# A graph kernel's first gathers, moved from the start of message passing into the attention answers

## The chip, the cores and the metric

The kernel runs on 1 core of one Trainium2 chip. The metric is the device time of the core in microseconds; lower is better. TensorE is called PE in the profile (its weight loads PEld), VectorE is DVE, ScalarE is ACT, GpSimd is POOL, and SP is the engine that issues the plain transfers.

## The reference, cut to what matters

One layer on 3125 nodes with 256 channels: a layer norm, then a graph network and an attention-like mix of the normalised rows, both added to the input, then a feed-forward part with two of eight experts for each row. The part that the change touches is the message passing of the graph network, for three edge types t and three steps i:

```python
xn = _layernorm(x)
h = xn                                   # one state for each edge type
for i in range(3):
    m = h @ W[i]
    msg = m[src] * emask[:, None]        # 50000 edges, sorted by dst; emask picks type t
    agg = segment_sum(msg, dst, num_segments=3125)
    h = _gru_cell(agg, h, wih, whh, bih, bhh)
```

and the mix, of which only its place in time matters here: products of pairs of query components, multiplied with moments of keys and values, divided by their norm, and projected.

## The kernel before, in words

The kernel is a sequence of blocks; in a block each engine has its own list of instructions, and the blocks are parted by barriers of all engines. `mix_moments` normalises the rows, writes them to the table `xn_rows` in HBM as two f16 halves (a high and a low one, 512 numbers a row), keeps their transpose in SBUF as `xnT`, sorts out the edges (`idx0`, `idx1` hold the row of each edge's source, `keys` its destination and type) and makes the moments. `mix_answers` then makes the answers, in 14 units (7 groups of 448 nodes, two halves of the channels). SP loads 17 shifted copies of the queries for each unit into `R` (three buffers, each in four pieces, L831), VectorE multiplies them (L169), TensorE multiplies the products with the moments (L868, L877, L882, L891). `xnT` is not read any more in `mix_answers`, and GpSimd has nothing to do there.

`gnn` does three steps. In each, the edges are handled in batches of 256 (two gathers of 128 rows). A batch goes like this: GpSimd gathers the rows of the sources into a slab of `ring` (L1443; 12 slabs of two gathers); VectorE makes a one-hot matrix of the destinations in a window of 48 nodes, for the three types (L1288); TensorE multiplies rows with one-hot, eight short f16 matmuls (`count_batch`, L1114) into one of three PSUM banks; VectorE adds the bank into `agg` at the window's place (L1285). There are 195 such batches in a step, and before them a counted loop for edges that do not fit a window (`pe_pre`, `dve_pre`; one round with one batch for this input; its gathers are L1436, into a thirteenth slab). So that the message can be summed before it is multiplied with the weights, wih and W are multiplied with each other first, in four products for each type (`pe_products`, L1142; ScalarE copies them out, L1149).

The order of TensorE's work is written out ahead by `gate_plan`: which batches come before which matmul of the GRU units (L1191). A step begins with what is called the lead here: product of type 0, the counted loop, product of type 1, batches 0 to 2, product of type 2, batches 3 to 8. Then 48 units follow, with the other batches between their matmuls; the first matmul of unit 0 that reads `agg` waits for the adds of batches 0 to 8. A batch can't be added before the batch ahead of it, and TensorE starts batch b after the add of batch b - 3.

GpSimd's list in `gnn` is: for each step the counted loop's gathers, then the batches in order. Before batch b it waits, from the thirteenth of the kernel on, until TensorE is done with the batch twelve before:

```python
for b in range(MB):
    if s * MB + b >= SLABS:
        e.wait_ge(S["batch"], s * MB + b - SLABS + 1)
```

Of the kernel before, what the change touches and what calls it, by code (L numbers as in the profile page):

```python
# [5 lines left out]
F32 = mybir.dt.float32  # L6
# [10 lines left out]
P = 128  # L17
# [75 lines left out]
def gps_layer_kernel(nc, A):  # L93
# [44 lines left out]
    edges = {"keys": keys, "bases": bases, "main_at": main_at, "shift": shift, "idx0": idx0, "idx1": idx1, "tab": tab}  # L138
    with nc.sbuf_tensor("acc_mix", [PT, TILES, C], F32) as acc:
        with nc.sbuf_tensor("xnT", [P, KC, NP], F32) as xnT:  # L140
            mix(nc, A, acc, xnT, ident, ones, acc_rows, edges, table0, hT0)
    gnn(nc, A, tables, [hT0] + hTs, idx0, idx1, keys, bases, main_at, shift, tab, iota_keys, ident, acc_rows, xf)
    ffn(nc, A, acc_rows, ident, ones, xf, out)


def mix(nc, A, acc, xnT, ident, ones, acc_rows, edges, rows_to, cols_to):

    q_cols = nc.dram_tensor("q_cols", [KC, P + P // 2, NP], F32).ap()
    with ExitStack() as ctx:
        def sb(name, shape, dt=F32):  # L150
            return ctx.enter_context(nc.sbuf_tensor(f"mix_{name}", shape, dt))
        K = {"W": sb("W", [P, KC * PLACES, QUAD, HD]), "M": sb("M", [P, KC * PLACES, VD]), "same_head": sb("same_head", [P, QUAD]),
             "window": sb("window", [P, P + P // 2]), "vsum": sb("vsum", [P, KC]), "count": sb("count", [P, 1]),
             "bias3": sb("bias3", [3, 3 * C], BF16), "ones3": sb("ones3", [3, P], BF16),
             "R0": sb("R0", [P, ND, GW]), "square0": sb("square0", [P, GW])}
        mix_moments(nc, A, acc, xnT, ident, ones, q_cols, K, edges, rows_to, cols_to)
        mix_answers(nc, A, acc, q_cols, K, acc_rows)

# [633 lines left out]

def mix_answers(nc, A, acc, q_cols, K, acc_rows):

    with ExitStack() as ctx:
# [24 lines left out]
        with nc.Block() as block:  # L820
            @block.sync
            def _(e):
# [14 lines left out]
                while parked < GROUPS:  # L837
                    park(parked)
                    parked += 1
                e.wait_ge(S["parked"], 16 * GROUPS)  # L840

            @block.tensor
# [177 lines left out]

def gnn(nc, A, tables, cols, idx0, idx1, keys, bases, main_at, shift, tab, iota_keys, ident, acc_rows, xf):

    with ExitStack() as ctx:
# [9 lines left out]
        bi, bh, brz = (sb(name, [P, TYPES, 6]) for name in ("bi", "bh", "brz"))  # L1033
        ring = sb("ring", [P, SLABS + 1, BATCH, 2 * C], F16)
        onehot = sb("onehot", [P, 4, BATCH, NKEY], F16)
# [29 lines left out]
        col_store = [sem(f"g_col_store{t}") for t in range(TYPES)]  # L1065
        landed = [nc.alloc_semaphore(f"g_landed{r}") for r in range(SLABS)]
        V = [{n: sem(f"g{s}_pre_{n}") for n in ("idx", "paced", "onehot", "batch", "added", "now", "seen", "set", "done")} for s in range(STEPS)]
# [40 lines left out]

        def count_batch(e, pg, slab, hot, start_sem):
            for c in range(BATCH):  # L1110
                for part in range(2):
                    for k in range(KC):
                        o = part * C + k * P
                        mm = e.matmul(pg[:, k * TYPES:(k + 1) * TYPES, :].rearrange("p t d -> p (t d)"), ring[:, slab, c, o:o + P], hot[:, c, :],  # L1114
                                      start=(c == 0 and part == 0 and k == 0), stop=(c == BATCH - 1 and part == 1 and k == KC - 1), skip_group_check=True)
            mm.then_inc(start_sem, 1)

        def pe_pre(e, s):
            rounds, number = pre_rounds(e)
            with e.Fori(0, rounds) as r:  # L1120
                with e.Fori(0, number) as b:
                    e.wait_ge(V[s]["onehot"], r * NB + b + 1)
                    e.wait_ge(pre_landed[s], r * (16 * BATCH * NB) + b * (16 * BATCH) + 16 * BATCH)
                    count_batch(e, pagg[0], SLABS, onehot[:, 0, :, :], V[s]["batch"])

# [37 lines left out]
        def pe_range(e, s, first, end):  # L1163
            for b in range(first, end):
                e.wait_ge(S["onehot"], s * MB + b + 1)
                if b >= BANKS:
                    e.wait_ge(S["added"], s * MB + b - BANKS + 1)
                e.wait_ge(landed[b % SLABS], landings(s, b))
                count_batch(e, pagg[b % BANKS], b % SLABS, onehot[:, b % 4, :, :], S["batch"])

# [252 lines left out]
        with nc.Block() as block:  # L1423
            @block.gpsimd
            def _(e):
                rounds, number = pre_rounds(e)
                for s in range(STEPS):
# [3 lines left out]
                    with e.Fori(0, rounds) as r:  # L1431
                        with e.Fori(0, number) as b:
                            e.wait_ge(V[s]["idx"], r * NB + b + 1)
                            e.sem_inc(V[s]["paced"], 1)
                            for c in range(BATCH):
                                e.indirect_dma_start(ring[:, SLABS, c, :], None, tables[s], bass.IndirectOffsetOnAxis(ap=pre_idx[:, c:c + 1], axis=0)).then_inc(pre_landed[s], 16)  # L1436
                    idx = idx1 if s else idx0
                    for b in range(MB):
                        if s * MB + b >= SLABS:
# [515 lines left out]
```

## Time and profile before

| | us |
|---|---|
| median of 3 runs | 3063.77 (3057.07 to 3064.43) |
| the profiled execution, its own time | 3079.78 |
| its span | 3078.1 |
| TensorE busy | 2647.3 (86%) |
| VectorE busy | 1593.7 (52%) |
| GpSimd busy | 1334.5 (43%) |
| ScalarE busy | 642.6 (21%) |
| the answers: first and last instruction | 312.9 to 568.1 |
| `gnn`: first instruction | 572.2 |
| first gather of step 0, of step 1, of step 2 | 584.0, 1233.2, 1882.1 |
| first instruction of the feed-forward part | 2541.1 |

Times in a timeline are microseconds from the span's start. In each row stand start, duration, engine, line and operation, output and inputs, the number of instructions merged into the row, and in brackets how long the engine sat idle before it and what released it; "issue" means that the profile shows nothing it waited for, "remote" that the releaser could not be named. Some matmul records are missing from the trace.

### The profile page before, as it was taken

The numbers are of one execution on the slowest core, as the hardware profiler recorded it, in microseconds if no ns is written. First come the engines' busy times: TensorE is split into PE (matmuls) and PEld (weight loads), VectorE is DVE, ScalarE is ACT, GpSimd is POOL, SyncE is SP. The second block draws the span as 40 slices with busy tenths as digits, with TensorE's granted clock in tenths as the row PEclk, the third lists the DMA queues.
The fourth block names the chain that finished last, engine by engine and source line by source line (L and its number), as shares of the span: only waits on it lengthen the run. The fifth ranks groups of instructions, "written<-read, shape, count | busy, mean of one in ns | idle before, by whom it ended". The sixth has DMA issues, their size and how long they took to land. (4 is left out here: it accounts for less than half of the span.)

```text
span 3078.1 us, 39296 instructions
## 1 busy us (share of the span) xinstructions
PE 2647.3 (86%) x13041; PEld 1704.6 (55%) x13041; DVE 1593.7 (52%) x3119; ACT 642.6 (21%) x1180; POOL 1334.5 (43%) x1375
## 2 busy tenths in 40 slices
PE   5898899669988989688999897798898875899997
PEld 3434455355555556454555555654445455788886
DVE  6798877335555555254555552466667684111110
ACT  3211100111111114111111114122212231333222
POOL 0000000356666661666666643666666600333433
PEclk8898999879999999799999998899999995999998
DMA  4300765434444442444444434433444413133223
GB/s 128 130 1 1 263 238 192 152 91 131 142 143 130 143 125 86 142 127 128 128 142 144 130 105 139 131 114 113 128 129 122 122 50 113 32 89 90 65 63 71
DMA packets 201473, 362.85 MB, mean 118 GB/s; under 512 B 27937, under 2 KB 156109, under 8 KB 201104
## 3 DMA queue, kind: packets, MB, share of 16 engines
q0 software_dynamic: 67776, 169.95, 20.1%
q1 hardware_dynamic: 129564, 186.48, 18.1%
q10 hardware_dynamic: 3956, 4.19, 0.5%
q8 instruction: 95, 1.56, 0.2%
q14 instruction: 82, 0.67, 0.1%
HBM read 293.37 MB, written 70.34 MB: 118 GB/s over the span
## 5 line engine op out<-in xcount | busy, mean ns | idle before, releaser
L1443 POOL DMA_INDIRECT g_ring<-h_rows,idx x780 | 768.2, 985 | 400.9 <-issue 199.3
L1114 PE MATMUL g_pagg<-g_onehot,g_ring 128*128 128x144 f16 x4704 | 425.7, 231 | 196.5 <-issue 187.8
L1114 PEld LDWEIGHTS g_pagg<-g_onehot,g_ring 128*128 128x128 f16 x4704 | 343.3, 100 | 452.7 <-issue 433.6
L1285 DVE TENSOR_TENSOR g_agg<-g_agg,g_pagg 128x288 f32 x585 | 265.4, 454 | 402.0 <-remote 233.1
L1443 POOL DMA_INDIRECT g_ring<-xn_rows,idx x390 | 386.6, 991 | 197.7 <-issue 102.3
L1288 DVE SCALAR_TENSOR_TENSOR g_onehot<-iota_keys,shift,keys 128x288 f16<-128x288 f16 x585 | 299.6, 513 | 0.6 <-issue 0.6
L1191 PE MATMUL g_pr<-g_agg,g_wc 128*128 128x448 f32 (+1 forms) x576 | 231.5, 524 | 15.2 <-issue 9.5
L1377 DVE SCALAR_TENSOR_TENSOR g_t<-g_ph,g_bh,g_rT 128x448 f32<-128x448 f32 (+1 forms) x144 | 89.9, 624 | 290.4 <-remote 209.2
L1191 PE MATMUL g_pz<-g_agg,g_wc 128*128 128x448 f32 (+1 forms) x576 | 230.8, 523 | 1.8 <-issue 1.7
L1191 PE MATMUL g_pr<-g_hT,g_wh 128*128 128x448 f32 (+1 forms) x576 | 226.0, 513 | 6.4 <-issue 6.3
L1191 PE MATMUL g_pz<-g_hT,g_wh 128*128 128x448 f32 (+1 forms) x576 | 221.6, 505 | 9.3 <-issue 6.3
L1191 PE MATMUL g_ph<-g_hT,g_wh 128*128 128x448 f32 (+1 forms) x576 | 224.0, 512 | 2.6 <-issue 2.5
L1191 PE MATMUL g_pi<-g_agg,g_wc 128*128 128x448 f32 (+1 forms) x576 | 222.8, 509 | 2.6 <-issue 2.5
L1239 ACT ACTIVATE g_nT<-g_t,g_bi 128x448 f32<-128x448 f32 (+1 forms) x144 | 89.7, 623 | 646.6 <-DVE g_t L1384 401.8
L1921 DVE TENSOR_TENSOR f_ys<-f_bank,f_b 128x256 f32<-128x256 f32 x58 | 24.6, 425 | 381.1 <-PE f_bank L1870 319.5
L1870 PE MATMUL f_bank<-f_w,f_hid 128*128 128x256 f32 x928 | 207.9, 382 | 6.0 <-ACT f_hid L1892 6.0
L1862 PE MATMUL f_bank<-f_slotsT,f_w 128*128 x928 | 207.7, 382 | 1.0 <-ACT f_slotsT L1885 1.0
L1436 POOL DMA_INDIRECT g_ring<-xn_rows,g_pre_idx x2 | 2.1, 1074 | 465.3 <-DVE g_pre_idx L1264 465.0
L1870 PEld LDWEIGHTS f_bank<-f_w,f_hid 128*128 128x128 f32 x928 | 173.9, 190 | 35.2 <-issue 12.7
L1862 PEld LDWEIGHTS f_bank<-f_slotsT,f_w 128*128 128x128 f32 x928 | 178.1, 192 | 26.0 <-issue 1.4
L1235 ACT ACTIVATE g_rT<-g_pr,g_brz 128x448 f32<-128x448 f32 (+1 forms) x144 | 84.5, 587 | 416.2 <-remote 281.8
L1892 ACT ACTIVATE f_hid<-f_bank,f_b 128x256 f32<-128x256 f32 x232 | 108.9, 474 | 247.0 <-PE f_bank L1862 246.8
(353 smaller groups left out, 3409.2 us busy)
## 6 DMA issues: line engine op xcount, KB each, us to landing
ma_R<-q_cols SPq DMA_DIRECT2D x27, 896.0 KB, 9.8
f_w<-in_L_ffn_W SPq DMA_DIRECT2D x16, 1024.0 KB, 7.7
h_cols<-g_hn SPq DMA_DIRECT2D x36, 448.0 KB
h_rows<-g_rows SPq DMA_DIRECT2D x36, 448.0 KB
g_hT<-h_cols SPq DMA_DIRECT2D x36, 448.0 KB
mix_R<-q_cols SPq DMA_DIRECT2D x15, 896.0 KB, 10.0
g_ring<-h_rows,idx POOLq DMA_INDIRECT x780
ma_R<-q_cols SPq DMA_DIRECT2D x9, 1120.0 KB, 5.6
```

What stands on the lines that cost most here:

```text
L1114: mm = e.matmul(pg[:, k * TYPES:(k + 1) * TYPES, :].rearrange("p t d -> p (t d)"), ring[:, slab, c, o:o + P], hot[:, c, :], start=(c == 0 ...
L1191: mm = e.matmul(p[:, 0:W], w, x, start=(first and k == 0), stop=(final and k == KC - 1), skip_group_check=True)
L1235: e.activation(rT[:, 0:W], pr[:, 0:W], ACT.Sigmoid, bias=brz[:, t, m:m + 1]).then_inc(S["r"], 1)
L1239: e.activation(nT[:, 0:W], t1[:, 0:W], ACT.Tanh, bias=bi[:, t, 4 + m:5 + m]).then_inc(S["n"], 1)
L1285: e.tensor_tensor(agg[:, :, bass.ds(o, DT)], agg[:, :, bass.ds(o, DT)], pagg[b % BANKS][:, :, :], ALU.add).then_inc(S["added"], 1)
L1288: e.scalar_tensor_tensor(out=onehot[:, b % 4, :, :], in0=iota_keys[:, :].unsqueeze(1).to_broadcast([P, BATCH, NKEY]), scalar=shift[:, 0:1] ...
L1377: e.scalar_tensor_tensor(out=t1[:, 0:W], in0=ph[:, 0:W], scalar=bh[:, t, 4 + m:5 + m], in1=rT[:, 0:W], op0=ALU.add, op1=ALU.mult).then_inc ...
L1443: e.indirect_dma_start(ring[:, b % SLABS, c, :], None, tables[s], bass.IndirectOffsetOnAxis(ap=idx[:, o:o + 1], axis=0)).then_inc(landed[b ...
L1862: mm = e.matmul(p1[m % 4], w1[:, x % 2, k, m * P:(m + 1) * P], slotsT[:, k, bass.ds(t * ST, ST)], start=(k == 0), stop=(k == KC - 1))
L1870: mm = e.matmul(p2[c], hid[:, m, c * P:(c + 1) * P], w2[:, x % 2, m, :], start=(m == 0), stop=(m == HC - 1))
L1892: e.activation(hid[:, m, :], p1[m % 4], ACT.Gelu, bias=b1[:, x, m:m + 1]).then_inc(S["hidden"], 1)
L1921: e.tensor_tensor(ys[:, c, :], p2[c], b2[:, x, :], ALU.add).then_inc(S["plain"], 1)
```

## The change

The first twelve batches of step 0 (24 gathers) are issued by GpSimd in `mix_answers`, in place of the start of `gnn`, and the block of the answers ends with a wait for their landing. The ring of twelve slabs now lies in the memory of `xnT`, which is kept allocated until the end of `gnn`; the slab of the counted loop becomes a tensor of its own, `pre_ring`. In `gnn`, step 0 begins its gathers with batch 12.

```diff
+    landed = [nc.alloc_semaphore(f"g_landed{r}") for r in range(SLABS)]
+    with nc.sbuf_tensor("xnT", [P, KC, NP], F32) as xnT:
+        ring = xnT[:, :, :].rearrange("p k n -> p (k n)").bitcast(F16)[:, 0:SLABS * BATCH * 2 * C].rearrange("p (r b c) -> p r b c", r=SLABS, b=BATCH)
+        with nc.sbuf_tensor("acc_mix", [PT, TILES, C], F32) as acc:
+            mix(nc, A, acc, xnT, ident, ones, acc_rows, edges, table0, hT0, ring, landed)
+        gnn(nc, A, tables, [hT0] + hTs, idx0, idx1, keys, bases, main_at, shift, tab, iota_keys, ident, acc_rows, xf, ring, landed)
...
+            @block.gpsimd
+            def _(e):
+                for b in range(SLABS):
+                    for c in range(BATCH):
+                        o = FIRST + (b + 1) * BATCH + c
+                        e.indirect_dma_start(ring[:, b, c, :], None, rows_from, bass.IndirectOffsetOnAxis(ap=idx0[:, o:o + 1], axis=0)).then_inc(landed[b], 16)
+                for b in range(SLABS):
+                    e.wait_ge(landed[b], 16 * BATCH)
...
-        ring = sb("ring", [P, SLABS + 1, BATCH, 2 * C], F16)
+        pre_ring = sb("pre_ring", [P, BATCH, 2 * C], F16)
...
-                    count_batch(e, pagg[0], SLABS, onehot[:, 0, :, :], V[s]["batch"])
+                    count_batch(e, pagg[0], pre_ring, onehot[:, 0, :, :], V[s]["batch"])
...
-                count_batch(e, pagg[b % BANKS], b % SLABS, onehot[:, b % 4, :, :], S["batch"])
+                count_batch(e, pagg[b % BANKS], ring[:, b % SLABS, :, :], onehot[:, b % 4, :, :], S["batch"])
...
-                                e.indirect_dma_start(ring[:, SLABS, c, :], None, tables[s], bass.IndirectOffsetOnAxis(ap=pre_idx[:, c:c + 1], axis=0)).then_inc(pre_landed[s], 16)
+                                e.indirect_dma_start(pre_ring[:, c, :], None, tables[s], bass.IndirectOffsetOnAxis(ap=pre_idx[:, c:c + 1], axis=0)).then_inc(pre_landed[s], 16)
                     idx = idx1 if s else idx0
-                    for b in range(MB):
+                    for b in range(0 if s else SLABS, MB):
```

## Rows read from the trace of the kernel before

**Rows 1.** The page, costliest groups: line, operation, tiles, count | busy, mean ns | idle before.

```profile
L1443 POOL DMA_INDIRECT g_ring<-xn_rows,idx x390 | 386.6, 991 | 197.7 <-issue 102.3
```

**Rows 2.** Waits from 586 to 1194: who waited for whom, us in total, times, longest.

```profile
POOL g_ring L1443 <- remote: 48.6, 30, 4.1
POOL g_ring L1443 <- PE g_pagg L1114: 46.9, 27, 6.7
...
PEld g_pagg L1114 <- DMA g_ring<-xn_rows,g_pre_idx: 7.0, 1, 7.0
```

**Rows 3.** Timeline of GpSimd at the start of step 0.

```profile
584.03 1.18 POOL L1436 DMA_INDIRECT g_ring<-xn_rows,g_pre_idx  x1 [464.98 <-DVE g_pre_idx L1264]
...
586.78 0.96 POOL L1443 DMA_INDIRECT g_ring<-xn_rows,idx  x1 [0.31 <-issue]
...
626.35 0.95 POOL L1443 DMA_INDIRECT g_ring<-xn_rows,idx  x1 [4.07 <-remote]
```

**Rows 4.** Timeline of TensorE, lead of step 0.

```profile
599.77 1.66 PE L1114 MATMUL g_pagg<-g_onehot,g_ring 128*128 128x144 f16 x24
601.27 1.50 PE L1142 MATMUL g_pr<-g_hn 128*128 128x384 f32 x4
...
605.19 1.45 PE L1142 MATMUL g_pz<-g_hn 128*128 128x384 f32 x4
...
623.30 0.30 PE L1114 MATMUL g_pagg<-g_onehot,g_ring 128*128 128x144 f16 x1 [0.44 <-issue]
624.70 0.28 PE L1114 MATMUL g_pagg<-g_onehot,g_ring 128*128 128x144 f16 x1 [1.09 <-issue]
...
640.11 1.86 PE L1191 MATMUL g_pr<-g_agg,g_wc 128*128 128x224 f32 x4 [3.18 <-DVE g_agg L1285]
```

**Rows 5.** Timeline of VectorE and ScalarE, same stretch.

```profile
604.40 0.45 DVE L1285 TENSOR_TENSOR g_agg<-g_agg,g_pagg 128x288 f32 x1 [7.57 <-remote]
604.77 0.51 DVE L1288 SCALAR_TENSOR_TENSOR g_onehot<-iota_keys,shift,keys 128x288 f16<-128x288 f16 x1
...
626.17 0.49 ACT L1149 ACTIVATE g_wc<-g_pr 128x384 f32<-128x384 f32 x1 [25.71 <-remote]
626.21 0.45 DVE L1285 TENSOR_TENSOR g_agg<-g_agg,g_pagg 128x288 f32 x1 [11.06 <-remote]
```

**Rows 6.** Timeline, lead of step 1.

```profile
1269.78 0.45 DVE L1285 TENSOR_TENSOR g_agg<-g_agg,g_pagg 128x288 f32 x1 [20.79 <-remote]
...
1269.92 0.95 POOL L1443 DMA_INDIRECT g_ring<-h_rows,idx  x1 [4.16 <-remote]
...
1289.59 1.86 PE L1191 MATMUL g_pr<-g_agg,g_wc 128*128 128x224 f32 x4 [2.52 <-DVE g_agg L1285]
```

**Rows 7.** Timeline, lead of step 2.

```profile
1918.75 0.45 DVE L1285 TENSOR_TENSOR g_agg<-g_agg,g_pagg 128x288 f32 x1 [20.84 <-remote]
...
1918.89 0.95 POOL L1443 DMA_INDIRECT g_ring<-h_rows,idx  x1 [4.19 <-remote]
...
1935.93 1.02 PE L1191 MATMUL g_pr<-g_agg,g_wc 128*128 128x224 f32 x4 [1.31 <-issue]
```

**Rows 8.** Stretches: length, busy of PE, PEld, DVE, ACT, POOL, clock, DMA share, GB/s.

```profile
313.00:345.00 32.00, 28.14 (x70) 13.72 (x71) 31.68 (x17) 1.79 (x3) 0.00 (x0) 0.95 0.99 374
...
610.00:615.00 5.00, 0.79 (x3) 0.34 (x4) 0.73 (x2) 0.00 (x0) 3.78 (x5) 0.50 0.36 105
699.00:1194.00 495.00, 446.81 (x2328) 256.96 (x2327) 267.65 (x547) 86.07 (x139) 313.73 (x316) 0.98 0.43 131
```

**Rows 9.** Timeline, VectorE and TensorE early in the answers.

```profile
322.11 5.89 DVE L169 TENSOR_TENSOR ma_R<-ma_R 128x1792 f32<-128x1792 f32 x3
...
338.45 1.02 PE L882 MATMUL ma_pz<-ma_R,ma_T 128*128 128x448 f32 x2 [3.42 <-DVE ma_T L918]
339.30 6.18 PE L868 MATMUL ma_py<-ma_R,mix_W 128*128 128x448 f32 x16
```

**Rows 10.** Line L1413 from 699 to 1194: count, ns min/median/max, first and last start.

```profile
L1413 DVE TENSOR_TENSOR g_hn<-g_dT,g_nT x35: 617/620/627, 707.5 to 1186.5; 128x448 f32<-128x448 f32 x35
```

More of the change, by code:

```diff
@@ L138, in gps_layer_kernel, with mix @@
     edges = {"keys": keys, "bases": bases, "main_at": main_at, "shift": shift, "idx0": idx0, "idx1": idx1, "tab": tab}
[L139 to L142, printed above, removed]
+    landed = [nc.alloc_semaphore(f"g_landed{r}") for r in range(SLABS)]
[4 more added lines that the diff above has]
+        gnn(nc, A, tables, [hT0] + hTs, idx0, idx1, keys, bases, main_at, shift, tab, iota_keys, ident, acc_rows, xf, ring, landed)
     ffn(nc, A, acc_rows, ident, ones, xf, out)
-def mix(nc, A, acc, xnT, ident, ones, acc_rows, edges, rows_to, cols_to):
+def mix(nc, A, acc, xnT, ident, ones, acc_rows, edges, rows_to, cols_to, ring, landed):
     q_cols = nc.dram_tensor("q_cols", [KC, P + P // 2, NP], F32).ap()
@@ L156, in mix @@
         mix_moments(nc, A, acc, xnT, ident, ones, q_cols, K, edges, rows_to, cols_to)
-        mix_answers(nc, A, acc, q_cols, K, acc_rows)
+        mix_answers(nc, A, acc, q_cols, K, acc_rows, edges["idx0"], rows_to, ring, landed)
 def turned_queries(q_cols, u, a, b):
@@ L790, in _, with mix_answers @@
                 e.tensor_scalar(K["count"][:, :], pm[3][:, HEADS // 2:HEADS // 2 + 1], 16 * SC ** 4, None, ALU.mult)
-def mix_answers(nc, A, acc, q_cols, K, acc_rows):
+def mix_answers(nc, A, acc, q_cols, K, acc_rows, idx0, rows_from, ring, landed):
     with ExitStack() as ctx:
@@ L1018, in batches_needed, with gnn @@
     return MB if g == NG - 1 else PLAN[GPU * NU * g] - (KEPT if g else 0)
-def gnn(nc, A, tables, cols, idx0, idx1, keys, bases, main_at, shift, tab, iota_keys, ident, acc_rows, xf):
+def gnn(nc, A, tables, cols, idx0, idx1, keys, bases, main_at, shift, tab, iota_keys, ident, acc_rows, xf, ring, landed):
     with ExitStack() as ctx:
@@ L1065, in gnn @@
         col_store = [sem(f"g_col_store{t}") for t in range(TYPES)]
-        landed = [nc.alloc_semaphore(f"g_landed{r}") for r in range(SLABS)]
         V = [{n: sem(f"g{s}_pre_{n}") for n in ("idx", "paced", "onehot", "batch", "added", "now", "seen", "set", "done")} for s in range(STEPS)]
@@ L1107, in pre_rounds, with count_batch @@
             return rounds, number
-        def count_batch(e, pg, slab, hot, start_sem):
+        def count_batch(e, pg, rows, hot, start_sem):
             for c in range(BATCH):
@@ L1113, in count_batch @@
                         o = part * C + k * P
-                        mm = e.matmul(pg[:, k * TYPES:(k + 1) * TYPES, :].rearrange("p t d -> p (t d)"), ring[:, slab, c, o:o + P], hot[:, c, :],
+                        mm = e.matmul(pg[:, k * TYPES:(k + 1) * TYPES, :].rearrange("p t d -> p (t d)"), rows[:, c, o:o + P], hot[:, c, :],
                                       start=(c == 0 and part == 0 and k == 0), stop=(c == BATCH - 1 and part == 1 and k == KC - 1), skip_group_check=True)
```

## The prediction

> **What bounds the kernel now.** I read the page first, then the waits of step 0, then its start engine by engine. GpSimd issues 390 gathers in step 0 at a mean of 991 ns, and sits idle 197.7 us between them [rows 1]. So the first question is whether anybody waits for a gather. In the waits of step 0, GpSimd waits for TensorE: 46.9 us under TensorE's name and 48.6 us under "remote", which are waits for a free slab of the ring. TensorE's weight loads for the batches wait for a gather once, 7.0 us, and that is the preliminary gather, not one of the ring [rows 2]. The ring is ahead of its reader from the first batch: batch 0's rows are issued from 586.78 [rows 3] and its matmuls start at 599.77 [rows 4]. A head start of twelve batches therefore buys nothing as data that arrive sooner.
>
> The second question is what happens in the lead of step 0, between that first gather and the first matmul that reads `agg`, at 640.11 [rows 4]. TensorE executes batches 0 to 2 (24 matmuls) from 599.77 and the third weight product from 601.27, and then its matmuls come singly, once or several times 0.7 us apart (623.30, 624.70) [rows 4]. VectorE's adds of batches 0 and 2, which need only those batches and each other, come at 604.40 and 626.21, after waits of 7.57 and 11.06 us, and ScalarE copies a product bank out after a wait of 25.71 us [rows 5]. TensorE has done the work; the others learn of it up to 25 us late. I call this the late retirement.
>
> What ends it is visible on GpSimd. It issues without a pause until the ring is full, sits idle 4.07 us, from 622.28, and at 626.35 goes on [rows 3]. The same picture stands in the leads of steps 1 and 2: idle 4.16 and 4.19 us, and the release at once in all engines, VectorE's first add at 1269.78 and 1918.75 after 20.79 and 20.84 us of waiting [rows 6, 7]. Three leads, three times some 4.1 us after the last gather: I take it that an unbroken stream of gathers holds TensorE's retirement back, and that its stop lets it go. The ring starts empty in each step, so that GpSimd can issue 26 to 28 gathers before it must stop. That is what the change alters.
>
> **The change, part by part.**
>
> (a) Moved gathers. 24 gathers (twelve batches of two) leave the start of step 0 and are issued at the start of the answers, from about 313. At 0.96 us each and 0.30 us between them [rows 3] they take 24 x 1.26 = 30.3 us on GpSimd, which was idle for 464.98 us before its first gather of the kernel before [rows 3]. So their issue costs nothing, and the new wait for `landed` behind them ends long before the answers do; nothing of GpSimd's is queued behind it but the block's end. The price is on the DMA engines. From 313 to 345 these are busy 0.99 of the time at 374 GB/s with the loads of R [rows 8]. Gathers alone, in 610 to 615, take 0.36 of the engines [rows 8]: 24 of them are 30.3 x 0.36 = 10.9 us of all engines. VectorE is busy 31.68 of 32 us there [rows 8] and its products of unit 1 (three in 5.89 us from 322.11 [rows 9]) need the four pieces of R1. R1 is 3.9 MB, from 315 at 374 GB/s about 10.4 us, so its last piece is there at about 325 and is wanted at 322.11 + 3.93 = 326.0. With 0.36 of the engines taken away the same bytes need 10.4 / 0.64 = 16.3 us: 331.3, or 5 us late. VectorE then makes table T later, for which TensorE already waits 3.42 us at 338.45 [rows 9], so the lateness reaches the path. After that R2 and R3 have the margin of the unit behind them. Cost +5 us; at least 0 (gathers that get less than their share), at most the whole 10.9.
>
> (b) 586 to 600 without ring gathers. The preliminary gather, for which TensorE waits 7.0 us [rows 2], shares the engines with weights and four ring gathers. Those are 0.52 MB; at 374 GB/s 1.4 us. I take -1; the bounds are 0 and -7.0, the whole wait.
>
> (c) The lead. GpSimd now finds the ring full after the two preliminary gathers, and is silent from about 586.5 until batch 0 is done, at 599.77 + 0.7 = 600.5. A stream that does not run cannot hold batches 0 to 2 back. From there on things stand as they stood in steps 1 and 2 at the release: batches 0 to 2 just retired, the third product still in hand, GpSimd starting again. In step 1 it is 1289.59 - 1269.78 = 19.8 us from the first add to the first matmul on `agg`, in step 2 1935.93 - 1918.75 = 17.2 us [rows 6, 7]. Here it would come at 600.6 + 19.8 = 620.4 or 617.8 in place of 640.11: 19.7 or 22.3 us, taken as -21. The least is 0 (retirement late for another reason). The most is a lead with no late retirement at all: products end at 605.19 + 1.45 = 606.6 [rows 4], six batches at VectorE's 0.45 + 0.51 us for add and one-hot [rows 5] are 5.8 us, unit 0 reads `agg` at 612.4: -28.
>
> (d) What follows. From 699 to 1194 TensorE is busy 446.8 of 495 us, its clock granted at 0.98 [rows 8], and GpSimd follows it a ring's length ahead as before. So what the lead gains is kept to the end. Steps 1 and 2 issue what they did. The ring's new address, the name `pre_ring` and the order of the semaphores cost nothing.
>
> Sum: +5 - 1 - 21 = -17 us. The profiled execution took 3079.8 (span 3078.1); it would take 3062.8. Its time is 16.0 us above the median of the three runs. If late retirement were the profiler's own doing, these 16 us would have to hold all three leads of some 20 us each; so I take most of it as real and carry -17 over: 3063.8 - 17 = 3046.8, say 3047.
>
> **Rivals.**
>
> First rival, slower: the late retirement belongs to TensorE, not to the gathers. For it: in each step it follows the counted loop `pe_pre`, and it holds TensorE's short f16 matmuls first. Against it: the constant 4.1 us after the last gather, and after 699 the same f16 matmuls run with gathers beside them in a stretch in which TensorE is 90% busy. Then only (a) and (b) are left, +4 us with 0 to 11 as bounds: 3068. It decides if VectorE's first adds in step 0 still wait 7 us and more. The Trainium skill has a rule that points this way: in "Runtime: NRT & Kernel Launch", instruction fetch mechanics, a taken branch out of the prefetched window is said to force a fetch before execution goes on. By that rule the stall would stay where the loop ends. The trace does not agree well: the release falls with the gathers' pause, not at a place in the code.
>
> Second rival, a smaller gain: the stall re-forms. GpSimd starts at 600.6 and has a slab for each retired batch, so batches 3 to 8 run beside a stream again. A slab is two gathers, 2.5 us; a stall with three slabs of runway lasts at most 7.6 us plus the 4.1. One such stall beyond what steps 1 and 2 show costs 11.7: -17 + 11.7 = -5: 3058.
>
> Third rival: the late retirement appears in the answers. 24 gathers in one stream there are as many as in a lead, and no full ring breaks them. A pair of weight load and matmul takes 6.18 / 16 = 0.39 us there [rows 9]; at 0.7 us per instruction it would take 1.4. From ten us after the first gather to 4 us after the last, 323 to 347, that loses 24 x (1 - 0.39 / 1.4) = 17 us: the sum is 0, 3064. Against it: it began each time at a burst of f16 matmuls (24 in 1.66 us [rows 4]), and this stretch has none.
>
> Fourth rival: GpSimd and VectorE get in each other's way in the answers. VectorE has no idle time there; if each gather held it for its 0.96 us, 23 us would be added: 3070. The trace speaks against it: 35 adds of two SBUF operands took 617 to 627 ns each where gathers run beside them two thirds of the time [rows 8, 10]. The Trainium skill ("SBUF — State Buffer", two separate sides) has that lock for VectorE's two-input operations against a GpSimd operation that reads SBUF. By that rule VectorE would lose time here; the rows show none.
>
> **How the numbers follow.** My forecast holds with 0.62, its own range being 3039 to 3056 (from -25 to -8, the bounds of (a) and of (c) against each other). Second rival 0.15, first 0.13, third 0.07, fourth 0.03. The range that leaves 2 in 10 out reaches into the first rival's (3064 to 3075) and past my own below: 3037 to 3066. The three runs lie 7.4 us apart, so 0.3%, 9.2 us, is about the least that can be told from no change; the limit is 3054.6. Nearly all of my forecast lies below it (0.58), with a little of the second rival: faster 0.62. Same takes the rest of those two, the third and most of the first: 0.29. Slower 0.09.
>
> **What would show it.** Right: in step 0 no gathers between the preliminary ones and about 600; VectorE's first three adds within a few us of 600; the first matmul on `agg` 17 to 20 us after the first of them; TensorE's wait at table T of unit 1 some 5 us longer. Wrong: adds that still come 10 us apart with GpSimd silent (first rival), a GpSimd idle of 4.1 us with everything released behind it at about 612 (second), or matmuls 0.7 us apart between 323 and 347 (third). The forecast is also wrong if unit 0 starts early and the time is given back before 699.

## The result and the profile after

| | before | after |
|---|---|---|
| median, us | 3063.77 (3057.07 to 3067.44, 5 runs) | 3035.57 (3032.14 to 3044.5, 5 runs) |
| profiled execution, us | 3079.78 | 3038.09 |
| its span, us | 3078.1 | 3036.4 |

The ratio of the medians is 0.9911, with a 95% interval of 0.9895 to 0.9926: 28.2 us faster. That is the direction forecast. The time is 11.4 us below the 3047 forecast, and 1.4 us below the lower end of the range (3037). The two profiled executions differ by 41.7 us. That of before was 16.0 us above its median and that of after 2.5, so 13.5 us of the 41.7 are the choice of executions. Every comparison of the two profiles below carries that uncertainty. All line numbers behind the answers are ten higher in the changed kernel (the batches' matmuls are L1124, the adds L1295, the ring's gathers L1453), and the ring now appears under the name `xnT`.

First the lead of step 0, the timelines of GpSimd, TensorE and VectorE in the kernel after:

```profile
586.66 0.96 POOL L1446 DMA_INDIRECT g_pre_ring<-xn_rows,g_pre_idx  x1 [0.30 <-issue]
602.17 0.96 POOL L1453 DMA_INDIRECT xnT<-xn_rows,idx  x1 [14.55 <-PE g_pagg L1124]
```

```profile
592.90 1.14 PE L1124 MATMUL g_pagg<-g_onehot,g_pre_ring 128*128 128x144 f16 x8 [5.26 <-DMA g_pre_ring<-xn_rows,g_pre_idx]
...
601.24 1.66 PE L1124 MATMUL g_pagg<-g_onehot,xnT 128*128 128x144 f16 x24
...
611.61 2.94 PE L1124 MATMUL g_pagg<-g_onehot,xnT 128*128 128x144 f16 x24 [2.00 <-issue]
...
617.55 1.02 PE L1201 MATMUL g_pr<-g_agg,g_wc 128*128 128x224 f32 x4 [1.76 <-DVE g_agg L1295]
```

```profile
602.03 0.45 DVE L1295 TENSOR_TENSOR g_agg<-g_agg,g_pagg 128x288 f32 x1 [4.43 <-PE g_pagg L1124]
...
602.91 0.46 DVE L1295 TENSOR_TENSOR g_agg<-g_agg,g_pagg 128x288 f32 x1
...
611.05 0.46 DVE L1295 TENSOR_TENSOR g_agg<-g_agg,g_pagg 128x288 f32 x1 [6.41 <-PE g_pagg L1124]
```

GpSimd is silent for 14.55 us, as forecast, and starts again as soon as batch 0 is done. VectorE adds batch 0 at 602.03, 0.79 us after TensorE starts the three batches, where before it waited 7.57 us [rows 5]. From the first batch to the first matmul on `agg` it is 617.55 - 601.24 = 16.3 us, against 640.11 - 599.77 = 40.3 [rows 4]: 24.0 us gone.

The lead of step 1, where nothing was changed, looks as before [rows 6]: VectorE's first add comes after 20.69 us (20.79 before) and GpSimd goes on 0.14 us later, after 4.04 us (4.16).

```profile
1245.30 0.46 DVE L1295 TENSOR_TENSOR g_agg<-g_agg,g_pagg 128x288 f32 x1 [20.69 <-remote]
...
1245.44 0.95 POOL L1453 DMA_INDIRECT xnT<-h_rows,idx  x1 [4.04 <-remote]
```

In the answers VectorE's operations took as long as before, and the gathers took longer. GpSimd's timeline, then VectorE's:

```profile
312.48 4.59 POOL L849 DMA_INDIRECT xnT<-xn_rows,idx  x1 [194.44 <-POOLq L88]
317.38 0.97 POOL L849 DMA_INDIRECT xnT<-xn_rows,idx  x1 [0.30 <-issue]
...
331.28 4.82 POOL L849 DMA_INDIRECT xnT<-xn_rows,idx  x1 [0.30 <-issue]
```

```profile
325.60 2.03 DVE L171 TENSOR_TENSOR ma_R<-ma_R 128x1792 f32<-128x1792 f32 x1 [0.73 <-DMA ma_R<-q_cols]
...
331.12 4.15 DVE L928 TENSOR_TENSOR ma_pairs<-mix_window,mix_M 128x2176 f32<-128x2176 f32 x1
```

The last piece of R1 is waited for 0.73 us, where the forecast had 5. From 313 to 345 only 13 gathers got through, not 24, and the engines moved 390 GB/s with them instead of the 374 of [rows 8]:

```profile
313.00:345.00 32.00, 27.60 (x66) 13.12 (x65) 31.17 (x16) 1.79 (x3) 28.28 (x13) 0.92 1.02 390
```

The clock differs there too (0.92 against 0.95). After its wait for table T, TensorE gets the 1.2 GHz level for 3.4 us in the kernel after, and stays at 2.4 GHz in the kernel before. The same matmuls, after and then before:

```profile
338.80:342.20 3.40, 3.40 (x6) 1.41 (x6) 3.40 (x4) 0.00 (x0) 3.10 (x2) 0.50 1.05 407
```

```profile
339.40:342.80 3.40, 3.40 (x11) 1.73 (x10) 3.40 (x4) 0.00 (x0) 0.00 (x0) 1.00 1.05 405
```

Last, where TensorE stood still. Each row below is the group of the batches' matmuls in one step, in the order step 0, step 1, step 2. The number behind the second bar is TensorE's idle time before them. The rows are cut at 1180 and 1830 us; a few matmuls of the kernel before fall into the next row by that, but cut at the ends of its steps the idle times are the same. Before:

```profile
L1114 PE MATMUL g_pagg<-g_onehot,g_ring 128*128 128x144 f16 x1523 | 140.9, 232 | 72.4 <-issue 65.5 <-DMA g_ring<-xn_rows,g_pre_idx 6.4
...
L1114 PE MATMUL g_pagg<-g_onehot,g_ring 128*128 128x144 f16 x1575 | 141.4, 230 | 57.3 <-issue 56.2 <-DVE g_onehot L1288 0.5
...
L1114 PE MATMUL g_pagg<-g_onehot,g_ring 128*128 128x144 f16 x1613 | 144.1, 232 | 66.8 <-issue 66.1
```

and after:

```profile
L1124 PE MATMUL g_pagg<-g_onehot,xnT 128*128 128x144 f16 x1560 | 138.0, 230 | 45.8 <-issue 45.3
L1124 PE MATMUL g_pagg<-g_onehot,g_pre_ring 128*128 128x144 f16 x8 | 1.1, 324 | 5.3 <-DMA g_pre_ring<-xn_rows,g_pre_idx 5.3
...
L1124 PE MATMUL g_pagg<-g_onehot,xnT 128*128 128x144 f16 x1560 | 139.1, 228 | 46.7 <-issue 45.6
...
L1124 PE MATMUL g_pagg<-g_onehot,xnT 128*128 128x144 f16 x1560 | 138.8, 231 | 62.2 <-issue 62.0
```

Step 0 lost 72.4 - 45.8 - 5.3 = 21.3 us of idle. Steps 1 and 2 lost 10.6 and 4.6 more, though no instruction of theirs was changed; these are waits that the profile can't name, in single executions. They are not gaps in the trace: it holds all 4704 matmuls of the batches, in both kernels. VectorE's first multiplication with a reset gate dates the gain. It comes at 621.7 against 643.9 in step 0 (22.2 us sooner), in the last group of step 0 at 1174.7 against 1198.5 (23.8), and in the last group of step 2 at 2454.2 against 2495.8 (41.6). Between these the lead comes and goes: 28.6 us at the start of step 1, 33.1 at its end, 29.8 at the start of step 2.

### The profile page after: what moved, and what is told of

It reads as the page before. It is cut to its first block and busy times, and to the rows that moved or that the text cites. A ratio compares the mean times of both kernels' runs of the same rounds, so it can differ in the third digit from the quotient of the medians.

```text
span 3036.4 us, 39301 instructions
## 1 busy us (share of the span) xinstructions
PE 2646.3 (87%) x13041; PEld 1701.2 (56%) x13041; DVE 1592.0 (52%) x3119; ACT 642.5 (21%) x1180; POOL 1358.7 (45%) x1375
## 3 DMA queue, kind: packets, MB, share of 16 engines
q0 software_dynamic: 67776, 169.95, 20.2%
## 5 line engine op out<-in xcount | busy, mean ns | idle before, releaser
L1453 POOL DMA_INDIRECT xnT<-h_rows,idx x780 | 775.2, 994 | 378.0 <-issue 206.6
L1124 PEld LDWEIGHTS g_pagg<-g_onehot,xnT 128*128 128x128 f16 x4680 | 337.1, 99 | 408.3 <-issue 396.3
L1124 PE MATMUL g_pagg<-g_onehot,xnT 128*128 128x144 f16 x4680 | 416.0, 230 | 154.8 <-issue 152.8
L1295 DVE TENSOR_TENSOR g_agg<-g_agg,g_pagg 128x288 f32 x585 | 265.1, 453 | 370.6 <-remote 159.6
L1453 POOL DMA_INDIRECT xnT<-xn_rows,idx x366 | 360.6, 985 | 198.8 <-issue 95.0
L1830 POOL DMA_INDIRECT acc_rows<-f_ys,f_past x58 | 93.0, 1604 | 139.6 <-DMA acc_rows<-f_ys,f_past 87.9
```

The lines of the kernel that those rows point to most:

```text
L1295: e.tensor_tensor(agg[:, :, bass.ds(o, DT)], agg[:, :, bass.ds(o, DT)], pagg[b % BANKS][:, :, :], ALU.add).then_inc(S["added"], 1)
L1453: e.indirect_dma_start(ring[:, b % SLABS, c, :], None, tables[s], bass.IndirectOffsetOnAxis(ap=idx[:, o:o + 1], axis=0)).then_inc(landed[b ...
L1830: e.indirect_dma_start(acc_rows, bass.IndirectOffsetOnAxis(ap=past[:, c:c + 1], axis=0), ys[:, c, :], None, compute_op=ALU.add).then_inc(x ...
```

## The experiments

All twelve ran on three other chips than the one on which before and after were timed. On each of the three the kernel before takes 2792 to 2796 us, not 3064. So each experiment is to be read against the kernel before as timed beside it on the same chip, and first it has to be seen what is different there.

### The kernel before, seen again

Expected:

> The kernel before, profiled a second time, to see which of the 41.7 us between the two profiled spans are one execution's own. If the first profile of before was a slow execution in steps 1 and 2, this one is 10 to 16 us shorter than 3078 there, while the lead of step 0 (599.8 to 640.1, 40.3 us) stays 38 to 42 us. If steps 1 and 2 really are slower in the kernel before, this one repeats them within 3 us.

It took 2794.8 us beside a median of 2794.3. The answers take 256.1 us (314.2 to 570.3), near the 255.2 of the first chip. Message passing, 575.5 to 2251.7, is where the difference is. The same 86.5 us of a group of units on the first chip (862.7 to 949.2) take 72.6 us here. Both stretches, first chip and then this one:

```profile
862.70:949.20 86.50, 77.31 (x401) 44.67 (x400) 46.10 (x96) 14.99 (x24) 57.15 (x58) 0.96 0.45 137
```

```profile
811.80:884.40 72.60, 72.60 (x402) 43.17 (x400) 46.24 (x94) 14.53 (x24) 55.53 (x57) 1.00 0.53 161
```

The work is the same (some 400 matmuls, VectorE 46 us), but TensorE is busy all the time here and its clock is granted at 1.00, the 2.4 GHz level throughout, where the first chip left it idle for 9.2 us and granted 0.96, nearly all of it at that level. Over the whole run TensorE is busy 2555.4 us of 2793.1 here and 2647.3 of 3078.1 there: of the 285 us between the two spans 193 are more idle time of TensorE and 92 are matmuls that took longer. The late retirement is absent in the lead too. VectorE's timeline:

```profile
601.87 0.45 DVE L1285 TENSOR_TENSOR g_agg<-g_agg,g_pagg 128x288 f32 x1 [3.89 <-PE g_pagg L1114]
...
602.73 0.46 DVE L1285 TENSOR_TENSOR g_agg<-g_agg,g_pagg 128x288 f32 x1
...
603.59 0.46 DVE L1285 TENSOR_TENSOR g_agg<-g_agg,g_pagg 128x288 f32 x1
```

TensorE starts batches 0 to 2 at 601.07, and all three are added within 3 us, while GpSimd gathers without a pause: all 392 gathers of step 0, from 587.3 to 1094.2, have no gap between them above 0.3 us. An unbroken stream is thus not enough to make retirement late. In its place there is a wait that the first chip did not have. The waits of this kernel in step 0:

```profile
POOL g_ring L1443 <- issue: 113.7, 373, 0.3
PE g_pagg L1114 <- DMA g_ring<-xn_rows,idx: 11.5, 8, 2.0
POOL g_ring L1443 <- PE g_pagg L1114: 5.2, 17, 0.3
PE g_pagg L1114 <- DMA g_ring<-xn_rows,g_pre_idx: 3.9, 1, 3.9
```

The 5.2 us under TensorE's name are 17 gaps of at most 0.3 us, the ordinary gap between gathers, so GpSimd never waits for a free slab here. On the first chip it waited 95.5 us [rows 2]. TensorE waits eight times for a gather of the ring. A faster TensorE has made the gathers the late ones: two gathers of 0.95 us with 0.30 us between them are 2.5 us a batch. The first two of these waits are in the lead:

```profile
612.51 0.66 PE L1114 MATMUL g_pagg<-g_onehot,g_ring 128*128 128x144 f16 x8 [1.89 <-DMA g_ring<-xn_rows,idx]
614.78 1.12 PE L1114 MATMUL g_pagg<-g_onehot,g_ring 128*128 128x144 f16 x8 [1.61 <-DMA g_ring<-xn_rows,idx]
```

### The change, seen and timed again

Edit: none; the changed kernel as it is. Expected:

> The change once more, next to the kernel before on one chip. Two kinds of chip have shown up: one on which the kernel before takes 3064 us and TensorE's retirement is late in each lead, and one on which it takes 2794 us and is never late. On the second kind TensorE waits for the ring's gathers in batches 6 to 8 and 19 to 26 of step 0. Theory for that kind (the head start counts as data that arrive sooner, and six batches of it already do all of it): 2777 to 2781 us, as six batches gave 2778.7. Rival there (the more batches ahead the better): below 2772. On the first kind it repeats the change's 28 us, within 4 us.

2777.53 us (2773.82 to 2780.37) against 2793.35: ratio 0.9943 (0.9929 to 0.9956), 15.8 us. TensorE's waits for gathers of `xn_rows` into the ring fell from 11.5 us to 0.3:

```profile
PE g_pagg L1124 <- DMA g_pre_ring<-xn_rows,g_pre_idx: 6.0, 1, 6.0
PE g_pagg L1124 <- issue: 0.3, 2, 0.2
PE g_pagg L1124 <- DMA xnT<-xn_rows,idx: 0.3, 1, 0.3
```

Part of the rest is the clock. In the kernel before, among waits for gathers of 1.6 to 2.0 us, the clock is granted at 0.50 (1.2 GHz) from 614.5 to 617.9 and again in the stretch below; in the changed kernel it is 1.00 from 600 to the end of the step. The matmuls in these two stretches, 3.12 and 4.81 us, would take half at the higher level: an estimate of 4 us from these rows.

```profile
658.90:665.70 6.80, 4.81 (x20) 3.24 (x21) 0.00 (x0) 0.00 (x0) 5.28 (x6) 0.50 0.50 139
```

From the first instruction of `gnn` to the first reset gate of the last group it is 1088.5 - 575.1 = 513.4 us, against 1103.5 - 575.5 = 528.0. The answers take 256.1 us in both, and R1's last piece is waited for 0.57 us with the gathers and 0.56 without: here the gathers cost the answers nothing. The end of the block takes 0.4 us longer with them (5.4 us for 5.0 from TensorE's last matmul to `gnn`).

### How many batches ahead

Edit for six; for three it is `SLABS // 4`:

```diff
-                for b in range(SLABS):
+                for b in range(SLABS // 2):
...
-                    for b in range(0 if s else SLABS, MB):
+                    for b in range(0 if s else SLABS // 2, MB):
```

> The change with six batches gathered ahead instead of twelve; GpSimd issues the other six (12 gathers, 15 us) in the lead, from about 588 to 603, past the burst of batches 0 to 2 at 601. Theory: that stream is some 15 us old at the burst, as in the kernel before (16 us), so batches 0 to 2 retire late, but GpSimd stops at 603 for lack of a free slab and all is released 4 us later, at 607. That is 5 us later than in the change, in the shadow of the third product: 0 to 6 us slower than the change, 3035 to 3042. Rival (the stall has nothing to do with the stream): adds as prompt as in the change, no difference beyond 3 us.

> The changed kernel with three batches (6 gathers) issued in the answers in place of twelve; step 0 of message passing issues batches 3 to 11 itself. Theory 'data that arrive sooner': three batches are a lead of 3 x 2.5 = 7.6 us for every later gather of step 0. On a chip where the kernel before takes some 2794 us, its TensorE waits there about 14 us in all for gathers, so 7 to 8 us of them go: ratio 0.9973 (0.9965 to 0.998), half of what six and twelve batches give. Rival 'a fixed cost of starting the stream': any head start gives all of it: 0.9945. On a chip where the kernel before takes some 3064 us: by the theory of the late retirement GpSimd still issues 18 gathers without a pause (22.7 us) before the ring is full, so the lead keeps most of its stall and gains at most 7.6 us: ratio 0.9975 to 1.000; if TensorE itself is late, no change: 0.999 to 1.001.

Six: 2778.69 against 2794.3, ratio 0.9949 (0.9935 to 0.9962), 15.6 us. Three: 2786.76 against 2796.04, ratio 0.9964 (0.9952 to 0.9977), 9.3 us. Twelve give no more than six (15.8 us, on another chip), and three give rather more than half, a little more than the 7 to 8 us expected. The idle time before the batches' matmuls up to 700 says why. In the kernel before:

```profile
L1114 PE MATMUL g_pagg<-g_onehot,g_ring 128*128 128x144 f16 x312 | 26.9, 234 | 14.5 <-DMA g_ring<-xn_rows,idx 9.4 <-DMA g_ring<-xn_rows,g_pre_idx 3.9 <-DVE g_onehot L1288 1.1
```

with three batches ahead:

```profile
L1124 PE MATMUL g_pagg<-g_onehot,xnT 128*128 128x144 f16 x336 | 27.3, 228 | 3.7 <-DMA xnT<-xn_rows,idx 3.5 <-issue 0.2
```

9.4 us of waiting for gathers become 3.5 with three batches, and none of it is left with twelve. A fixed cost of starting the stream would have gone with any head start; this grows with the head start until nobody waits. So on these chips the rows that arrive sooner are what the change buys.

### A pause in the stream, without a head start

Edit, in the kernel before, for the three runs `before_pause0`, `before_pause0_b` and `before_pause0_c`. The run `before_pause_all` has `if b == 3` and `s * MB + 1` instead, and so the wait in all three steps:

```diff
                     for b in range(MB):
+                        if s == 0 and b == 3:
+                            e.wait_ge(S["batch"], 1)
```

GpSimd then waits ahead of batch 3's gathers until TensorE is done with batch 0. (The expectation of the third run calls this the counted loop's batch; it is batch 0 of the step.) Expected of the three runs of the same kernel:

> The kernel before with one wait more: in step 0, GpSimd stops before batch 3's gathers until TensorE is done with batch 0. No gather is moved, the rows of batches 3 to 11 come later than before. Theory (an unbroken stream of gathers holds TensorE's retirement back): VectorE's first adds come within 2 us of batches 0 to 2, the first matmul on agg at 617 to 624 instead of 640, and the time is 16 to 22 us below before, 3043 to 3048. Rival (the head start of twelve batches is what helps, or the stall belongs to the counted loop): the first adds come as late as before, 3062 to 3068 us.

> The kernel before, with GpSimd held in step 0 before batch 3's gathers until batch 0 is done; no gather moved. On a chip of the first kind: if the unbroken stream of gathers causes the late retirement, the first matmul on agg comes at 617 to 624 instead of 640 and the time is 12 to 22 us below before; if only the filled ring helps, within 4 us of before or slower. On a chip of the second kind there is nothing to cure, and it repeats 5 us more than before.

> The kernel before with one wait more: in step 0, ahead of batch 3's gathers, GpSimd waits until TensorE is done with the counted loop's batch. The same kernel as before_pause0, sent again for a chip where the kernel before takes some 3064 us. There, if the gather stream holds retirement back, the stream now stops after 8 gathers, VectorE's first adds of step 0 come within 2 us of TensorE's matmuls, and the lead ends some 10 to 20 us sooner: ratio 0.993 to 0.997. If TensorE itself is late (first rival), the adds still wait 7 us and more and the time stays or grows: 1.000 to 1.004. On a chip where the kernel before takes some 2794 us: 1.002 to 1.003, as measured twice.

Measured 2799.2, 2801.8 and 2799.92 us; ratios 1.0019 (1.001 to 1.0027), 1.0031 (1.0019 to 1.0044) and 1.0015 (1.0006 to 1.0024). In the first of the three profiles GpSimd stands still for 4.30 us (6.83 and 6.86 in the others), and what it issues next is late by that:

```profile
593.89 1.02 POOL L1445 DMA_INDIRECT g_ring<-xn_rows,idx  x1 [0.30 <-issue]
599.21 0.95 POOL L1445 DMA_INDIRECT g_ring<-xn_rows,idx  x1 [4.30 <-PE g_pagg L1114]
```

The loss, 4 to 8 us, is about that pause. From batch 0 to the first matmul on `agg` it is 20.2 to 20.7 us in the three profiles, against 16.2 without the pause. It confirms the gathers' pace as the bound of the start of step 0. The question for which the kernel was made, whether a pause releases a TensorE that retires late, can't be answered where none retires late.

> The kernel before; in each of the three steps GpSimd waits ahead of batch 3's gathers until TensorE is done with batch 0 of the step. On a chip where the kernel before takes some 2794 us: by the theory that the gathers' pace binds at the start of a step, the losses add up: some 6 us for step 0 (ratio 1.0015 to 1.003, three runs) and some 16 us for steps 1 and 2 together (what after_pause12 lost against the changed kernel), so 1.006 to 1.009. If the pace binds in step 0 only: 1.0015 to 1.003. On a chip where the kernel before takes some 3064 us: if the gather stream holds retirement back, all three leads lose their stall, 10 to 20 us each: 0.981 to 0.991; if TensorE itself is late, 1.000 to 1.009.

2815.89 against 2792.02, ratio 1.0077 (1.006 to 1.0094): the losses add up, as the pace theory says. In steps 1 and 2 TensorE now waits 42.5 us for gathers of the ring, 10.7 more than the kernel before (31.8):

```profile
PE g_pagg L1114 <- DMA g_ring<-h_rows,idx: 42.5, 34, 3.6
```

The same wait put into steps 1 and 2 of the changed kernel:

> The change, and in steps 1 and 2 GpSimd stops before batch 3's gathers until TensorE is done with batch 0 of the step. Theory: the late retirement of 18 to 20 us vanishes from both leads; batches 3 to 8 then wait for their rows (2.5 us each from about 1251), which gives part of it back: 10 to 18 us less in each step, 3000 to 3016 us in all. Rival 1 (the stall belongs to TensorE's counted loop): the adds of batch 0 still wait 20 us, and the later gathers make it worse, 3040 or more. Rival 2: the stall goes, but an unbroken stream through the first units, with a ring that is never full, brings it back there: 3030 to 3045.

2794.74 us, ratio 1.0002 (0.9994 to 1.0011) to the kernel before: what step 0 gained is lost again in steps 1 and 2. TensorE's waits for `h_rows` there are 43.0 us with the pause,

```profile
PE g_pagg L1124 <- DMA xnT<-h_rows,idx: 43.0, 34, 3.4
```

and 36.1 us without it, in the changed kernel, of a profiled execution each. These 6.9 us are only part of the 17 by which this kernel is slower than the changed one. The same two profiles show where most of it lies: from batch 0 to the first matmul on `agg` it is 20.3 us with the pause and 12.2 without in step 1, and 21.3 and 13.9 in step 2, together 15.4 us more. TensorE's waits without the pause:

```profile
PE g_pagg L1124 <- DMA xnT<-h_rows,idx: 36.1, 30, 3.4
```

### TensorE's counted loop as straight code

The first rival laid the late retirement on the loop. Edit in `pe_pre` of the kernel before; it leaves out that the loop can have more rounds than one, which this input doesn't need:

```diff
-            rounds, number = pre_rounds(e)
-            with e.Fori(0, rounds) as r:
-                with e.Fori(0, number) as b:
-                    e.wait_ge(V[s]["onehot"], r * NB + b + 1)
-                    e.wait_ge(pre_landed[s], r * (16 * BATCH * NB) + b * (16 * BATCH) + 16 * BATCH)
-                    count_batch(e, pagg[0], SLABS, onehot[:, 0, :, :], V[s]["batch"])
+            e.wait_ge(V[s]["onehot"], 1)
+            e.wait_ge(pre_landed[s], 16 * BATCH)
+            count_batch(e, pagg[0], SLABS, onehot[:, 0, :, :], V[s]["batch"])
```

> The kernel before with TensorE's counted loop written as straight code (it makes one round with one batch for this input, so the work is the same). On a chip of the first kind: if TensorE's branch causes the late retirement, it vanishes in all three leads and the time falls by 40 us or more; if the stream of gathers does, within 3 us of before. On a chip of the second kind: within 3 us of before, by both.

2794.26 against 2793.35, ratio 1.0002 (0.9993 to 1.0011). On this chip the loop costs nothing that can be measured; for the first chip it says nothing.

### The gathers later in the answers

Edit, in the changed kernel, and once more with six batches instead of twelve. GpSimd waits for the tenth count of TensorE's answers, some 70% through the block (488.87 in 309.2 to 565.4):

```diff
             def _(e):
+                e.wait_ge(S["y"], 10)
                 for b in range(SLABS):
```

> The change, with its 24 gathers held until ten of the fourteen units of the answers are done, where the loads of R have two units' margin. If the 2.7 us by which the answers grew are the gathers' share of the DMA engines at the crowded start, the answers are 2 to 3 us shorter here and the time 2 to 3 us below the change. If the 2.7 us are not theirs, no difference beyond 1 us. A loss of more than 3 us would mean that the gathers are not done when the block ends.

> The changed kernel with six batches ahead in place of twelve, and their gathers not at the start of the answers but behind S[y] of 10, two thirds through them. On a chip where the kernel before takes some 2794 us: six batches gave what twelve give and the later place gave 2 us more, so the two together give what after_late gave: 0.9938 (0.993 to 0.995). If those 2 us came from fewer gathers next to the loads of the first units and not from the place, six batches behind the first units give no more than that either; above 0.996 neither holds, and six batches would be too few once their issue is late. On a chip where the kernel before takes some 3064 us: 0.985 to 0.993.

2775.51 us, ratio 0.9938 (0.9924 to 0.9951), and 2776.37 us, ratio 0.994 (0.9923 to 0.9957). The gathers run from 488.87 on, at a mean of 1.27 us (25.34 us for 20), in a stretch in which the DMA engines are not full (0.82):

```profile
488.87 1.17 POOL L850 DMA_INDIRECT xnT<-xn_rows,idx  x1 [371.62 <-PE ma_py L880]
490.35 2.37 POOL L850 DMA_INDIRECT xnT<-xn_rows,idx  x1 [0.30 <-issue]
493.03 0.96 POOL L850 DMA_INDIRECT xnT<-xn_rows,idx  x1 [0.30 <-issue]
```

```profile
485.00:520.00 35.00, 35.00 (x101) 18.10 (x100) 25.15 (x17) 2.42 (x4) 25.34 (x20) 1.00 0.82 288
```

Both intervals overlap that of the change itself (0.9929 to 0.9956), so the 2.0 us between the medians (2775.51 and 2777.53) can't be told from no difference. The profiles agree: the answers take 256.2 us with the gathers late and 256.1 with them early.

## Why the prediction was right and wrong

Direction and place were right: the gain is in the lead of step 0. Its size was not.

**(a) Moved gathers: mis-sized.** Forecast +5. From the first instruction of the answers to that of `gnn` it is 262.0 us against 259.3: +2.7 in the two profiles. The share 0.36 of the DMA engines was taken for a demand that R1's bytes must yield to, and for 24 gathers in a row. In the profile 13 gathers fell into that stretch instead of 24, since most were stretched by VectorE's large operations, and the engines moved 390 GB/s instead of 374. R1 was late by 0.73 us and TensorE's wait for table T was 3.94 us against 3.42 [rows 9], so 0.5 of the 2.7 is placed there. Another 1.7 is the clock: behind that wait the same matmuls (L868, in the kernel after L879) run at the 1.2 GHz level in the kernel after and at 2.4 in the kernel before, as shown above. The last 0.5 is the end of the block.

Most of this is no work of the gathers. Of seven profiles of the kernel before and its variants, which gather nothing in the answers, three have the same fall of the clock, and a wait of 0.53 to 0.56 us for R1's last piece. They take 261.4 us from the start of the answers to `gnn`. Four lack the fall and take 259.4. The profile of before happened to be one of the four. Of the changed kernel's seven, six have the fall and take 261.4 to 262.1, and one lacks it and takes 259.8. Compared like with like, the moved gathers cost 0 to 0.7 us where +5 was forecast.

**(b) The preliminary gather: nothing.** It was forecast to come 1 us sooner. The time from `gnn`'s first instruction to batch 0 is the same to 0.1 us: 572.2 to 599.77, and 573.7 to 601.24.

**(c) The lead: mechanism of the forecast not shown, size -24.0 for -21.** The signs came: silence until 602, three adds within 3 us, and the first matmul on `agg` 15.5 us after the first add, a little under the 17 to 20 listed. It is nearer to the bound without any late retirement (-28) than to the picture of steps 1 and 2, from which the size was taken. A short stall was left (the 6.41 us wait at 611.05), so the second rival was seen in small. The lead takes 16.3 us here and 12.6 where nothing is late (the changed kernel on another chip), so the stall costs 3.7 us, 2.0 of it TensorE's idle time, and not 11.7. Counted from the 599.77 of [rows 4], 12.6 us is 612.4, the forecast's bound. The size of the lateness was read too large: the 25.71 us are ScalarE's idle time since 600.46, and the product whose bank it copies ended at 602.8, 23.4 us before the copy [rows 4, 5]. The cause given, that an unbroken stream of gathers holds retirement back, is now narrower: the kernel before has the same stream on other chips and retires at once. It needs something of the first chip besides. On that chip the stream still fits the leads, five with it, in two kernels (late until 3.9 to 4.2 us after its last gather), and one without (not late). The 4.1 us is no constant of the chip: at 671 to 682 of the kernel before TensorE's matmuls come singly or a few at a time again, beside twelve gathers without a pause, and the release follows the last gather after 2.31 us:

```profile
681.90 0.95 POOL L1443 DMA_INDIRECT g_ring<-xn_rows,idx  x1 [2.31 <-remote]
```

Whether the stream causes the lateness stays open, since no kernel that takes the stream away without a head start ran on that chip. Nor does any run show whether the recording of an execution has a part in it.

**(d) What follows: too small.** The rest was to stay as it was. Within step 0 the gain grew only from 22.2 to 23.8 us. The timed gain is 28.2, so some 4 us more came in steps 1 and 2. In the two profiles it is 17.8 us, 11.8 of them inside step 2, behind its lead. The profiles put their surplus into waits "issue" of TensorE in steps 1 and 2. On the other chips these steps are the same before and after: 484.7 and 485.4 us from the first reset gate to that of the last group in step 1. So the surplus, too, belongs to the first chip's unnamed waits. Whether it is the ring's new place or chance of single executions isn't settled; the five timed executions of either kernel lie 10 to 12 us apart.

**The step that failed** is the sizing of the sum's terms, -17 for -28.2. As read from the two profiles, (a) is +2.7 for +5, (b) 0 for -1 and (c) -24.0 for -21, together -21.3: 2.3 us of the miss are the mis-sized (a) and 3.0 the mis-sized (c), less 1.0 for (b). Of the remaining 6.9 us, 1.6 by the last group of step 0 (22.2 to 23.8) and some 4.4 in steps 1 and 2 are what (d) put at nothing. The last 0.9 is no work of the change: the answers began 1.2 us sooner in the profile after. With like compared with like (a) is near 0, and its miss 4 to 5 us. The range failed as well. Its lower end was set at -26.8, above the -28 that the text itself gave as the bound of (c), and the -25 to -8 called the bounds of (a) and (c) are not: the bounds of (a), (b) and (c) add up to a gain of 35 us at the most.

**"A head start buys nothing as data that arrive sooner"** held for that chip, where TensorE waited for no ring gather [rows 2], and was worded as if it were a property of the kernel. On the three chips where TensorE retires in time it is wrong: there the gain, 15.8 us, is these waits and the clock that goes with them. GpSimd's spare time was the first chip's own slowness: its waits for a free slab fell from 95.5 us to none.

**The rivals.** The first (TensorE or its loop is late by itself) would have left the adds of step 0 waiting 7 us and more; they waited for TensorE's start only. As a place in the code the loop has fallen; that TensorE is late for a reason of its own, which the stream only accompanies, has not. The Trainium skill's rule behind it, in "Runtime: NRT & Kernel Launch", instruction fetch mechanics, found no support: the loop stands in the changed kernel as before and step 0's adds are prompt, and without the loop the time on the other chips is the same (1.0002). The third (late in the answers) fell: +2.7 us in all, and not +17. Its sign did appear for a moment: five matmuls start 0.75 us apart, from 339.2 to 342.2. But TensorE is busy throughout at a clock of 0.50, so this is the clock and not late retirement. Of the fourth, the lock exists and works the other way. VectorE's multiplication of 4.15 us took as long before (4.13 and 4.15), but the gathers beside it were stretched, to 4.59 and 4.82 us. By the Trainium skill ("SBUF — State Buffer", two separate sides) the two lock each other out, and whichever starts first holds the ports for its whole instruction. The trace agrees: the two multiplications had started first, 0.59 and 0.16 us ahead of the gathers, and the gathers ended 1.04 and 0.83 us behind them, about a gather's own 0.95. The forecast read the rule as if VectorE had to be the one that waits, looked at 0.62 us operations [rows 10] and concluded that there was no lock.

## What to carry to other kernels

A head start for gathers is worth the time in which their reader would wait for them, and what the clock loses by these waits. Count it batch by batch, issue pace against reading pace, and not from who waits on average: six batches did here what twelve do. A producer's idle time is a margin only as long as its consumer is as slow as in that profile. Before a difference of 2 us between two profiles is given to a change, look whether the clock fell in one of them and not in the other. On the faster chips the gathers of steps 1 and 2 are where the next microseconds lie: TensorE still waits 36.1 us there, and rows of a step can't be had before the step ahead is done.

## What the runs showed of the hardware

- The same kernel takes 3064 us on one chip and 2792 to 2796 on three others. The answers differ by 1 us, message passing by some 290. On the slow one TensorE's results are known late (by 23.4 us in the lead of step 0), with gaps that the profile can't name; the cause is open.
- Gathers of 128 rows run 0.95 us with 0.30 us between them. Beside VectorE's 4.15 us multiplication of two SBUF operands they took 4.59 and 4.82 us, ending about 1 us behind it, and VectorE lost nothing.
- Gathers beside a loading stretch at 374 GB/s raised the rate to 390. The wait for the loads was 0.73 us with them and 0 without in the first pair of profiles, 0.57 and 0.56 in the second.
- TensorE's clock fell to 0.50 for 3.4 us behind a wait of 3.77 us in one execution of the kernel before (on another chip), and not behind one of 3.42 us in another. The two lengths of the same block, 259.4 and 261.4 us, differ by that.
